# Both pairs of the pass for the maxima between the scores of heads 0 and 1 and those of heads 2 and 3

## What is computed

```python
qkv = jnp.einsum('bsd,ed->bse', x, qkv_w) + qkv_b      # x: (1, 2048, 128) after a layernorm
scores = jnp.einsum('bhqe,bhke->bhqk', q, k) * scale   # 16 heads, 2048 x 2048
attn = jax.nn.softmax(scores, axis=-1)
out = jnp.einsum('bhqk,bhke->bhqe', attn, v)
```

## Time and profile before

| what | value |
|---|---|
| median of three runs | 1898.9 us (1897.99 to 1899.58) |
| the profiled execution, its own time | 1899.25 us |
| span of its profile | 1897.5 us |
| TensorE busy | 83% of the span |
| VectorE busy | 72% |
| ScalarE busy | 45% |
| GpSimd busy | 12% |

### The profile page before, as it was taken

How to read it: one execution, slowest core, us unless ns; L and a number is a source line. 1 busy time by engine, 2 the same in 40 slices (tenths; PEclk the granted TensorE clock), 3 DMA queues, 4 the chain that set the end, 5 groups by cost and what they waited for, 6 DMA issues and landing times. The chain is left out here.

```text
span 1897.5 us, 24346 instructions
## 1 busy us (share of the span) xinstructions
PE 1583.4 (83%) x8296; PEld 644.2 (34%) x8309; DVE 1369.9 (72%) x1951; ACT 861.6 (45%) x1494; POOL 224.1 (12%) x148
## 2 busy tenths in 40 slices
PE   6987469899899899899898799899995356489999
PEld 3433112222222222222221443356662122256665
DVE  5776888888888888888880477656656999746554
ACT  2433327777776777776777344322223100042222
POOL 2222400000000000000000022211101234301110
PEclk8998659999999999999999999999997667799999
DMA  6000310000100010000000000000000000000000
GB/s 168 1 0 1 114 24 8 8 8 25 23 8 6 17 27 8 8 17 16 2 2 2 1 0 0 0 1 0 0 1 0 0 0 0 1 0 6 6 2 10
DMA packets 31349, 24.81 MB, mean 13 GB/s; under 512 B 9036, under 2 KB 28280, under 8 KB 31256
## 3 DMA queue, kind: packets, MB, share of 16 engines
q1 hardware_dynamic: 31256, 23.59, 4.7%
HBM read 17.41 MB, written 4.19 MB: 11 GB/s over the span
## 5 line engine op out<-in xcount | busy, mean ns | idle before, releaser
L1363 DVE TENSOR_REDUCE mx<-ps 128x2 f32<-128x1024 f32 x512 | 619.7, 1225 | 138.9 <-PE ps L1260 127.4
L1299 PE MATMUL ps<-qa,ka 40*128 40x512 bf16 x1024 | 296.8, 386 | 78.8 <-ACT xn L1345 42.2
L1345 ACT ACTIVATE xT<-ps 128x512 f32<-128x512 f32 x512 | 277.8, 595 | 155.2 <-PE ps L1299 155.2
L1345 ACT ACTIVATE xn<-ps 128x512 f32<-128x512 f32 x512 | 277.8, 595 | 107.2 <-PE ps L1299 107.2
L1260 PE MATMUL ps<-ka,qa 40*128 40x512 bf16 x1024 | 248.4, 399 | 37.5 <-DVE mx L1363 24.9
L1299 PE MATMUL ps<-qb,kb 44*128 44x512 bf16 x1024 | 254.0, 383 | 0.0
L1299 PEld LDWEIGHTS ps<-qa,ka 40*128 40x128 bf16 x1024 | 72.9, 93 | 454.5 <-ACT xT L1345 206.4
L852 ACT ACTIVATE silu<-ps 128x512 f32<-128x512 f32 x144 | 85.3, 597 | 265.1 <-PE ps L825 261.8
L887 DVE TENSOR_TENSOR hid<-ps,silu 128x512 f32<-128x512 f32 x144 | 97.8, 690 | 90.4 <-PE ps L829 88.8
L825 PE MATMUL ps<-xT,ew 128*128 (+1 forms) x288 | 150.4, 604 | 6.4 <-PEq L1731 4.8
L815 PEld LDWEIGHTS ps<-ew,hid 128*128 128x128 f32 x1152 | 138.7, 192 | 30.6 <-issue 29.9
(11 more groups left out here) (240 smaller groups left out, 1793.9 us busy)
## 6 DMA issues: line engine op xcount, KB each, us to landing
qa<-q_parts SPq DMA_DIRECT2D x160, 16.0 KB
ew<-in_L_ffn_w_dram SPq DMA_DIRECT2D x2, 1024.0 KB
qb<-q_parts SPq DMA_DIRECT2D x128, 16.0 KB
kb<-k_parts SPq DMA_DIRECT2D x64, 32.0 KB
qb<-neg_turned SPq DMA_DIRECT2D x128, 6.0 KB
ka<-k_parts SPq DMA_DIRECT2D x30, 64.0 KB
wraw<-in_L_ffn_w_dram SPq DMA_DIRECT2D x3, 512.0 KB, 6.7
q_parts<-part SPq DMA_DIRECT2D x4, 384.0 KB, 2.7
```

Of the source, the lines that this page charges most:

```text
L1299: mm = nc.tensor.matmul(m.ps[:, S2_BANK[s], :], keys, (qa, qb)[part][r, qc, hp, :], start=(part == 0), stop=(part == 1))
L1345: nc.scalar.activation(ex[kt % P_RING][:, h, :], m.ps[:, S2_BANK[s], :], ACT.Exp).then_inc(exped, 1)
L1363: nc.vector.reduce_max(mx[:, 2 * hp:2 * hp + 2, qt, kc], m.ps[:, 2 * (i % 2):2 * (i % 2) + 2, :], AX.X)\
```

## The change

The second slot's pairs of each step are issued before `score(kt, 1)` and no longer after it. No instruction is added or taken away, and the waits of each stay as they are.

```diff
                     score(kt, 0)
                     ahead(2 * kt)
+                    ahead(2 * kt + 1)
                     score(kt, 1)
-                    ahead(2 * kt + 1)
                     if kt >= 1:
                         weigh(g, qc, kt - 1)
```

## The result

Four runs of the changed kernel have a median of 1869.61 us (1868.94 to 1874.27), beside 1899.24 us for the kernel before in as many runs. The ratio is 0.985 with a 95% interval of 0.9833 to 0.9867. The forecast was 1870.5 us. The profiled execution took 1869.63 us, with a span of 1867.9 us against 1897.5 us before, 29.6 us less.

A forecast was written before the change was run, and what follows sets the result against it. The bound was a 3.02 us loop of waits per ordinary step, no engine being full. 28.3 us from 14 periods plus 0.4 from the first unit, 28.4 taken for rounding, gave 1870.5 us from 1898.9; range 1862 to 1882.

The forecast's parts named there:

- The chain: Ordinary step: scores 0.64, exponential and release 0.65, other scores and second pair 0.75, weighing 0.98, a loop of 3.02 us.
- Ordinary steps: 12 of 16 steps in a unit, and step 15: each shortens by 0.22 us, 3.02 to 2.80.
- The moved pair costs nothing: Between the matmuls of heads 2 and 3: 0.41 us free of 0.63, and the pair needs 0.22.
- The moved pair doesn't wait for VectorE: In ordinary steps the reduction it needs is released at 3.28 us and the pair comes at 3.47, 0.19 to spare.
- Steps 4 and 11: Steps with three pairs: scores of heads 2 and 3 stand behind the third pair's wait, 3.89 us against 3.47, 0.42 more.
- Steps 12 and 15, exponentials, copies of the maxima: Step 12 stays at 2.80 us, step 15 saves 0.22, exponentials aren't late, the copies keep some 2.5 us, no stall.
- The 14 periods: Units of 49.55 us each save 13 x 0.22 - 2 x 0.42 = 2.02 us, 28.3 us in all.
- The first unit: Starts at the lower clock, where moving wins nothing; full clock taken from its step 4, saving 0.4 us.
- B: Rival: steps with three pairs cost nothing because the steps behind them catch up; 41.3 us go, 1857.6 us; chance 0.04.
- C: Rival: the pair sticks out of the gap before head 3 by 0.12 us, ordinary steps win 0.10; 1893 us; chance 0.06.
- D: Rival: third pair of steps 4 and 11 waits for the second reduction, 1.55 us more each; 1904 us; chance 0.04.
- E: Rival: no change, the 0.22 us goes back into another wait, for instance on VectorE; 1899 us; chance 0.04.

The follow-up runs named there:

- both_behind: The changed kernel with both pairs of a step put behind the scores of heads 2 and 3; 2112.18 us (one run).
- extra1: The changed kernel with the matmuls of every odd pair issued twice, on the same data into the same banks; 1879.96 us (one run).
- extra2: The changed kernel with the matmuls of every odd pair issued three times, on the same data into the same banks; 1901.85 us (one run).
- third_last: The changed kernel with the third pair of steps 4 and 11 put behind the scores of heads 2 and 3; 1860.78 us, 0.9794 of the kernel before.
- no_holes: The changed kernel with HOLE_SLOTS = 0, so no step has three pairs and step 12 has two; 1873.27 us, 0.9862 of the kernel before.
- spread: third_last with one pair in step 12, three in step 15 and two in all other steps; 1846.52 us, 0.9719 of the kernel before.

## Why the prediction was right, step by step

- **The chain.** An ordinary step was said to be a loop through the first exponential, with the second pair on it and the first in its shadow. Right: both_behind takes both pairs out of the shadow and pays 0.44 us; the change puts both in and reaches the step without pairs.
- **Ordinary steps: 0.22 us each.** Measured 3.024 to 2.806 as means of six steps in a row, 0.218.
- **The moved pair costs nothing.** Right, but the width was mis-stated: "of which head 2's own 0.22 remains needed" is what failed. extra1 and extra2 show all of the 0.63 us as usable, head 2's matmul running beside head 3's. It changed no term of the sum; it would have called a third pair there 0.03 us too much.
- **The moved pair doesn't wait for VectorE.** Right: no wait stands in front of it, and VectorE idles 0.45 us where 0.44 was worked out. The forecast of VectorE busy for about 85 of 100 us was too high (82.4), since it left out step 12 and the longer steps 4 and 11.
- **Steps 4 and 11: 0.42 us more.** Measured 0.43, by the wait that was named, and third_last removes it.
- **Steps 12 and 15, exponentials, copies of the maxima.** Step 12 is unchanged, step 15 saves 0.22, and no wait on a DMA lengthened a period: all 14 lie between 47.57 and 47.59 us. The last copy of the maxima was done 2.65 us ahead of the next unit (498.92 and 501.57), where 2.5 was worked out.
- **The 14 periods: 28.3 us.** Measured 27.6; each term is right to 0.01 us. About half of the difference is the rounding of 0.218 to 0.22, thirteen times per unit, and most of the rest the 0.43 in place of 0.42, twice per unit.
- **The first unit: 0.4 us.** Measured 2.4, when the shift of the mark is left out. From step 4 to step 12 it was 0.45, as worked out (25.09 us before, 24.64 after). Ahead of step 4, where the term took nothing, it was 2.0: step 4 started 15.92 us after the first score before the change (278.16) and 13.96 after it (274.88). The term took the clock's rise as fixed, and it came 4.5 us earlier. At the lower clock the moved pairs even cost 0.4 us: step 2 started 7.54 us after the first score before, 7.92 after. The first score was 1.3 us earlier by chance, and the later stages gave 1.7 back; no term held either. That the sum came within 1 us of the median is in part luck, by this cancelling, and the periods are the better test.
- **The rivals.** B (the triple steps cost nothing) falls by their 0.43 us each, C (the pair sticks out) by head 3 at 1.30 and by extra1, D (third pair behind the second reduction) by the third pair at 2.15, and E (a new wait) by the ordinary steps without one.

The Trainium skill's page "Perfetto Trace Analysis", section "Tensor Engine Instruction (MATMUL, LD_WEIGHTS)", says that a matmul's recorded end is an estimate. The trace agrees with it by extra2, where 0.66 us of matmul issue stands in a place that shows 0.26 us of recorded idleness before the change, at a cost of 0.01.

## What to carry to other kernels

Draw one step of a steady loop as a chain with starts, not with recorded ends, and find which work lies in the shadow of the wait for another engine; independent work belongs there, until the shadow is full. Before moving it, ask for every case of the loop, the odd ones too, whether it brings a wait of its own, because on an in-order queue that wait then holds the critical work behind it; here two such steps of 16 gave back 0.86 of 2.83 us. And a layout whose stalls gather in one place can lose to TensorE's clock what it won: 0.85 us per unit in no_holes, on top of 1.4 us of stalls. Look at the granted clock of several units, for it fell in some and not in others.

## What the hardware showed that I had not expected

- Two waits of 0.7 us within one step 13 of no_holes were followed by a granted clock of 0.50, and in both_behind a step with 1.90 of 3.00 us busy was followed by it too, and later there were 100 us at 0.50. In other units of the same two runs the same waits left it at 1.00. In the changed kernel the wait of 1.11 us in steps 4 and 11 had no such effect in either trace.
- Two reductions of VectorE that are both ready take 2.36 us together; started as the pairs came, 1.28 apart, 2.51 us.
- The stages of unchanged code behind the block took 841.3 and 841.4 us in two traces of the kernel before, 843.0 and 843.5 in two of the changed one, and 845.5 in spread. The granted clock differed in places (0.52 against 1.00 over the same 7 us), but not in the same places in both executions of the changed kernel.
